# Transposing the probabilities and x by DMA in an attention and feed-forward block, with the products with v between the Q and the K projection

## The reference

```python
x = x + layernorm(attention(layernorm(x), Wq, Wk, Wv, Wo))
x = x + layernorm(ffn(layernorm(x)))
```

## Time and profile before

| | |
|---|---|
| median of 3 runs | 2287.74 us (2286.65 to 2289.22) |
| the profiled execution's own time | 2287.41 us |
| its span, first to last instruction | 2285.6 us |
| TensorE (PE) busy | 2179.5 us, 95% |
| VectorE (DVE) busy | 1384.5 us, 61% |
| ScalarE (ACT) busy | 792.8 us, 35% |
| GpSimd (POOL) busy | 774.8 us, 34% |
| DMA queue of SP, share of 16 engines | 13.7% |

### The profile page before, as it was taken

The page is one execution under the profiler, slowest core; times in us unless marked ns, Lnnn a source line. Parts: engine busy times, 40 slices in busy tenths (PEclk is TensorE's granted clock), DMA queues, the critical chain, the costliest instruction groups (busy, mean ns, idle before and its releaser), DMA issues.

```text
span 2285.6 us, 35735 instructions
## 1 busy us (share of the span) xinstructions
PE 2179.5 (95%) x13184; PEld 1134.0 (50%) x13184; DVE 1384.5 (61%) x3327; ACT 792.8 (35%) x1829; POOL 774.8 (34%) x905
## 2 busy tenths in 40 slices
PE   3989999999999999999999998769999999999997
PEld 2445555555555555555555554434444444444443
DVE  6776676576676676576566575775555455555544
ACT  4544444444444444444444443431111111111111
POOL 0254545545455454554545544610000000000000
PEclk8999999999999999999999999879999999999999
DMA  7000010010010010000010020231121221212111
GB/s 290 2 28 15 19 42 15 20 42 10 26 42 10 24 34 19 25 29 24 16 37 24 10 88 10 85 114 63 49 93 37 93 74 48 82 38 91 38 56 37
DMA packets 31190, 108.73 MB, mean 48 GB/s; under 512 B 4161, under 2 KB 4161, under 8 KB 29986
## 3 DMA queue, kind: packets, MB, share of 16 engines
q1 hardware_dynamic: 31010, 106.34, 13.7%
HBM read 72.77 MB, written 33.55 MB: 47 GB/s over the span
## 4 chain that ended last, share of the span: by engine, by line
PE 91%; DVE 4%; issue 1%; POOL 1%; DMA 1%; ACT 1%; SPq 0%; POOLq 0%; DVEq 0%; ACTq 0%
PE ps L568 29%; PE ps L428 10%; PE ps L429 9%; PE ps L430 9%; PE ps L462 6%; PE ps L453 5%; PE ps L439 5%; PE ps L440 5%; PE ps L441 5%; PE ps L473 5%; PE ps L598 1%; PE ps L558 1%; PE ps L418 1%; POOL arena L1148 1%; DVE arena L719 1%
## 5 line engine op out<-in xcount | busy, mean ns | idle before, releaser
L1148 POOL TENSOR_TENSOR arena<-arena,row_inv 128x512 f32<-128x512 f32 (+3 forms) x512 | 358.3, 737 | 648.7 <-DVE row_inv L730 648.7
L428 PE MATMUL ps<-arena,region 128*128 128x512 f16 x1024 | 389.4, 380 | 0.0
L429 PE MATMUL ps<-arena,region 128*128 128x512 f16 x1024 | 388.5, 379 | 0.0
L430 PE MATMUL ps<-arena,region 128*128 128x512 f16 x1024 | 388.3, 379 | 0.0
L568 PE MATMUL ps<-region 128*128 128x512 f16 x1536 | 341.5, 383 | 8.2 <-ACT arena L1101 4.6
L815 DVE CUSTOM_DVE_ANT_0 arena<-ps,con,pow 128x512 f32<-128x512 f32 (+3 forms) x512 | 246.4, 547 | 161.5 <-PE ps L453 161.5
L568 PE MATMUL ps<-region,arena 128*128 128x512 f16 x1536 | 337.4, 379 | 0.0
L1063 ACT ACTIVATE arena<-arena,neg_max 128x512 f32<-128x512 f32 (+3 forms) x512 | 280.0, 548 | 98.3 <-DVE neg_max L815 98.3
L706 DVE TENSOR_TENSOR rotated<-ps,con 128x512 f32<-128x512 f32 x128 | 88.5, 691 | 267.2 <-PE ps L430 267.2
L568 PEld LDWEIGHTS ps<-region 128*128 128x128 f16 x1536 | 151.3, 99 | 186.5 <-issue 10.1
L568 PEld LDWEIGHTS ps<-region,arena 128*128 128x128 f16 x1536 | 149.1, 98 | 174.2 <-issue 0.8
(11 more groups left out here) (123 smaller groups left out, 2732.8 us busy)
## 6 DMA issues: line engine op xcount, KB each, us to landing
arena<-x SPq DMA_DIRECT2D x32, 512.0 KB, 3.8
attn_scratch<-o_st SPq DMA_DIRECT2D x64, 256.0 KB, 2.2
region<-attn_scratch SPq DMA_DIRECT2D x8, 2048.0 KB, 9.1
v_split<-x SPq DMA_DIRECT2D x32, 512.0 KB, 4.2
out<-v_split SPq DMA_DIRECT2D x32, 512.0 KB, 5.1
arena<-wv SPq DMA_DIRECT2D x4, 1024.0 KB, 13.7
region<-wq SPq DMA_DIRECT2D x4, 1024.0 KB, 18.8
arena<-wk SPq DMA_DIRECT2D x4, 1024.0 KB, 6.6
```

Of the source, the lines that this page charges most:

```text
L428: mm(o, w[:, k, 0, cols], xnt[par][:, k, 0, :], start=(k == 0), stop=False)
L429: mm(o, w[:, k, 0, cols], xnt[par][:, k, 1, :], start=False, stop=False)
L430: last = mm(o, w[:, k, 1, cols], xnt[par][:, k, 0, :], start=False, stop=(k == KT - 1))
L1148: gp.tensor_tensor(unit_sb(j, a), unit_sb(j, a), row_inv[:, n:n + 1].broadcast_to([PART, 128 * (j + 1)]), ALU.mult).then_inc(norm_done, 1)
```

## The change

P and x of the next batch are no longer transposed by TensorE. ACT writes the normalised probabilities' high half (the product with the inverse row sum, which carries the factor 2^14 now), DVE the low half, both as f16 in SBUF; SP then issues one transposing DMA of 128 x 2560 for each half into `pt`. POOL normalises nothing any more. For x, one tile is loaded at a time into `x_tile`, normalised, split, and each half transposed by a DMA. On TensorE the products with v of pair g-1 stand between the Q and the K projection and are cut at the query blocks of the new layout (36 instead of 24 matmuls over the same columns). The order of the query blocks changes. As `x_ring` gives room away, the chunks of W_O and W_F are loaded two at a time, and half of them a second time.

```diff
-Q_ORDER = (3, 2, 0, 1)
+Q_ORDER = (2, 0, 3, 1)
+PV_PIECES = {0: ((0, 2), (2, 2)), 1: ((1, 1), (2, 2)), 2: ((2, 2),), 3: ((3, 1),)}
...
 # SP, slot
+                if not last_b and 1 <= p <= ST:
+                    tok = slice(128 * (p - 1), 128 * p)
+                    for hl, src in enumerate((xn_high_t, xn_low_t[:, :])):
+                        sp.wait_ge(xn_split[hl], n)
+                        if p == 1 and hl == 0 and not first:
+                            sp.wait_ge(qk_done[1], PAIRS * b)
+                        sp.nop(nofuse=True)
+                        sp.dma_start_transpose(xnt[1 - bp][:, :, hl, tok], src).then_inc(xnt_in[hl], 16)
                 if not last_b and p < ST:
-                    sp.wait_ge(xt_done, 8 * b + 2 * p + 2)
-                    sp.dma_start(x_ring[:, p, :], x_v[b + 1, p]).then_inc(x_in[p], 16)
+                    if first and p == 0:
+                        sp.wait_ge(xt_done, 2 * ST)
+                    else:
+                        need(sp, xn_split[1], n)
+                    sp.dma_start(x_tile, x_v[b + 1, p]).then_inc(x_next_in, 16)
+                if not (first and p == 0):
+                    sp.wait_ge(pv_done, g)
+                for hl in range(2):
+                    sp.wait_ge(p_done[hl], 8 * g + 8)
+                    sp.nop(nofuse=True)
+                    sp.dma_start_transpose(pt[:, hl], p_split[:, hl].rearrange("p a n -> p (a n)")).then_inc(
+                        pt_in[hl], 16)
                 if not (first and p == 0):
                     sp.wait_ge(o_low, g)
...
 # TensorE, slot
-                need(pe, pt_low, NG * g)
+                need(pe, masked, 8 * g)
                 need(pe, o_low, g - 1)
                 score_products()
                 qk_product(0, n_pair, n_bp, range(KT), bank)
-                need(pe, masked, 8 * g + 8)
-                if not last_b and 1 <= p <= ST:
-                    need(pe, xn_done, 4 * b + 4 + p)
-                    for hh in range(2):
-                        x_transposes(p - 1, hh, BANK_XT[hh])
+                if not (first and p == 0):
+                    need(pe, masked, 8 * g + 8)
+                    need(pe, v_low, v_before(kind, p, b))
+                    for hl in range(2):
+                        need(pe, pt_in[hl], 16 * g)
+                    pv_products((p - 1) % PAIRS)
                 if has_qk:
                     need(pe, v_low, v_before(kind, p, b))
                     qk_product(1, n_pair, n_bp, range(KT), 1 - bank)
-                if not (first and p == 0):
-                    need(pe, v_low, v_before(kind, p, b))
-                    pv_products((p - 1) % PAIRS)
-                need(pe, norm_done, 8 * g + 8)
-                p_transposes()
...
 # DVE
+            def p_low_part(g, n):
+                j, a = UNITS[n]
+                need(dve, p_done[0], 8 * g + n + 1)
+                v.scalar_tensor_tensor(unit_p(j, a, 1), unit_sb(j, a), row_inv[:, n:n + 1], unit_p(j, a, 0),
+                                       ALU.mult, ALU.subtract).then_inc(p_done[1], 1)
...
                 inverse(g, 0)
+                if not last_b and 1 <= p <= ST:
+                    xn_low_part(4 * b + p - 1)
+                inverse(g, 1)
                 if has_qk:
                     qk_drain(0, g + 1, bank)
-                inverse(g, 1)
+                need(dve, pt_in[1], 16 * g)
+                for n in range(len(UNITS)):
+                    p_low_part(g, n)
                 if not last_b and p < ST:
-                    need(dve, x_in[p], 16 * (b + 2))
-                    ln_stats(p, 4 * b + 4 + p)
+                    need(dve, x_next_in, 16 * (4 * b + p + 1))
+                    ln_stats(p, 4 * b + 4 + p, x_tile)
-                if last_b and p < 2:
+                if last_b and p in (1, 2):
...
                 if has_qk:
                     qk_drain(1, g + 1, 1 - bank)
+                if not last_b and p < ST:
+                    ln_apply(p, 4 * b + 4 + p, x_tile)
+                if has_qk:
                     qk_low_part(0, g + 1)
                 if not (first and p == 0):
                     o_evac(g - 1, (p - 1) % 2)
-                for grp in range(NG):
-                    pt_evac(grp, g)
                 if has_qk:
                     qk_low_part(1, g + 1)
-                if not last_b and p < ST:
-                    ln_apply(p, 4 * b + 4 + p)
...
 # ACT, slot: after the exponentials
-                    for hh in range(2):
-                        xt_evac(p - 1, hh, 1 - bp, 8 * b + 8 + 2 * (p - 1) + hh, BANK_XT[hh])
+                need(act, pt_in[0], 16 * g)
+                for n in range(len(UNITS)):
+                    p_high_part(g, n)
...
-                for grp in range(NG):
-                    pt_evac(grp, g)
+                if not last_b and p < ST:
+                    xn_high_part(4 * b + p)
...
 # POOL, slot
-                for n in range(len(UNITS)):
-                    normalise(g, n)
```

More of the change, by code:

```diff
@@ L307, in unit_sb, with unit_p, raw_of @@
             return scores[:, a, S_OFF[j]:S_OFF[j] + 128 * (j + 1)]
+        def unit_p(j, a, hl):
+            return p_split[:, hl, a, S_OFF[j]:S_OFF[j] + 128 * (j + 1)]
+        def raw_of(w, c, again):
+            if w in w_raw:
+                return w_raw[w][:, KC * c:KC * (c + 1), :]
+            return raw_late[c + 2 if w == W_F and again else c % 2]
         block = ctx.enter_context(nc.Block())
@@ L377, in slot @@
                         store_o(b, p - 1, (p - 1) % 2)
+                if last_b and p == 0:
+                    for c in (0, 1):
+                        load_raw(W_O, c)
+                if last_b and p in (1, 6):
+                    w = {1: W_O, 6: W_F}[p]
+                    for c in (2, 3):
+                        sp.wait_ge(part_max_done, CHUNKS * {W_O: 1, W_F: 2}[w] + c - 1)
+                        load_raw(w, c)
+                if last_b and p == 4:
+                    for n in (0, 1):
+                        sp.wait_ge(w_low_done, CHUNKS * W_O + n + 1)
+                        load_raw(W_O, n, again=True)
+                if last_b and p == 5:
+                    for n in (0, 1):
+                        sp.wait_ge(w_low_done, CHUNKS * W_O + n + 3)
+                        load_raw(W_F, n)
+                if last_b and p == PAIRS - 1:
+                    phase2_loads()
             def batch(b, kind):
@@ L383, in _ @@
             over_batches(sp, batch)
+            for hl in range(2):
+                sp.wait_ge(pt_in[hl], 16 * PAIRS * B)
+            for c in (0, 1):
+                load_raw(W_F, c, again=True)
             sp.wait_ge(o_low, PAIRS * B)
@@ L541, in slot @@
                     if p >= 4:
-                        need(pe, xt_low, 8 * b + 8 + 2 * (p - 4) + 2)
+                        for hl in range(2):
+                            need(pe, xnt_in[hl], 16 * (4 * b + p - 3))
                     v_product(p % 4, 1 if p < 4 else 0, bp if p < 4 else 1 - bp, range(KT), bank)
@@ L549, in _ @@
             over_batches(pe, batch)
-            pe.wait_ge(pt_low, NG * PAIRS * B)
+            for hl in range(2):
+                pe.wait_ge(pt_in[hl], 16 * PAIRS * B)
             pe.wait_ge(o_low, PAIRS * B - 1)
@@ L729, in inverse @@
                 need(dve, exp_done, 8 * g + 4 * part + 4)
-                v.reciprocal(row_inv[:, 4 * part:4 * part + 4], row_sum[:, 4 * part:4 * part + 4]).then_inc(inv_done, 1)
+                four = slice(4 * part, 4 * part + 4)
+                v.reciprocal(row_rec[:, four], row_sum[:, four]).then_inc(recip_done, 1)
+                need(dve, recip_done, 2 * g + part + 1)
+                v.tensor_scalar(row_inv[:, four], row_rec[:, four], P_UP, None, ALU.mult).then_inc(inv_done, 1)
             dve.wait_ge(const_in, 32)
@@ L841, in slot @@
                 if last_b and p in (4, 5):
[L842 to L843 removed]
+                    for n in (0, 1):
+                        split_low(W_O, 2 * (p - 4) + n, LATE_ORDER[2 * (p - 4) + n])
                 if last_b and p >= 6:
@@ L1070, in slot @@
                         act.wait_ge(v_done, 8 * B)
-                    split_high(W_O, 2 * (p - 4))
-                    split_high(W_O, 2 * (p - 4) + 1)
+                    for n in (0, 1):
+                        split_high(W_O, LATE_ORDER[2 * (p - 4) + n], again=p == 5)
                 if has_qk:
@@ L1117, in step @@
                 if kind == 0:
-                    split_high(W_F, 2)
-                    split_high(W_F, 3)
+                    split_high(W_F, LATE_ORDER[2], again=True)
+                    split_high(W_F, LATE_ORDER[3], again=True)
             over_tiles(act, step)
```

153 lines of the change are left out of this document (68 added, 85 removed), and 5 rows, old and new, of the table PT_GROUPS.

## The result

The changed kernel takes 2325.32 us (median of four runs, 2323.25 to 2326.24); the kernel before, run beside it, 2287.19. The ratio is 1.0165, with a 95% interval of 1.0147 to 1.0182: **1.65% slower**, where a gain of 39 us was forecast. The profiled execution took 2325.03 us, its span 2323.2, and the mean granted clock of TensorE is 0.952, where it was 0.979.

A forecast was written before the change was run, and what follows sets the result against it. TensorE's instructions were taken as the bound, with K's tail right behind. Middle slots -53, batch 0 +11 and -6, last batch +4 and +5 sum to -39 us from 2287.41: 2248 us, range 2200 to 2320.

The forecast's parts named there:

- DVE, ACT, POOL: Work moved to these engines: low halves of P some 3.3 us on DVE, beside TensorE, ending at about 12 us.
- The x slots: Slots 0 to 3 of a batch: x work delays K's drain up to 1 us, adding 0.9 us, then 1.3.
- the forecast of the middle slots: Slots 8 to 55: mean slot 20.8 us, a gain of 1.1 us in each of 48, 53 us.
- The term for the clock: Batch 0, slots 0 to 3: after 6 us idle, scores run at the lower clock, 1.74 us more each.
- The tail of K: Drain to rounding and difference after K's product: 6.0 us, covered only by a 5.3 us V product, stalling TensorE 1 us.
- TensorE's own time: TensorE alone per slot: 21.92 less 2.33 and 0.55 for transposes, plus 0.15 for more v instructions, 19.2 us.
- Rival 1: TensorE stays the bound if K's tail is below 5.3 us: slots 19.2 us, about 2170 us; chance 5%.
- Rival 2: Work crowds ahead of K's drain, POOL starting K's rotation 1 us later each slot: about 2295 us; chance 20%.
- Rival 3: Transposing DMAs set the pace through slow small rows, from 8.7 us each: about 3110 or 4850 us; chance 15%.
- packet row: Evidence for slow transposing DMAs: the queue's mean packet of 162 ns, giving an upper bound of 25.8 us per transfer.
- The figure of 5 us: Assumed time of each 640 KB transposing DMA of P, near the plain x load; covered up to 8.7 us.
- The ends: First and last batches: +11 and -6 us in batch 0, +4 and +5 us in the last.

The follow-up runs named there:

- run 5: Changed kernel with v products behind the K projection, POOL's Q rotation after the low halves, x statistics behind K's drain: 2184.80 us, ratio 0.9551.
- run 1: Changed kernel with only the products with v put back behind the K projection: 2320.82 us, ratio 1.0145 to the kernel before.
- run 3: Changed kernel with the x work done in batch 0 alone, leaving out part of the computation: 2237.56 us, ratio 0.9776.
- run 7: Changed kernel with v products behind the K projection and x statistics behind K's drain, POOL still rotating Q beside the low halves: 2227.17 us.
- run 2: Changed kernel with POOL rotating Q only after the low halves of P are done: 2249.50 us, ratio 0.983.
- run 4: Changed kernel with x statistics behind K's drain, the root behind K's rotation, normalisation and high half of x later: 2231.30 us, ratio 0.9753.
- run 6: Changed kernel with Q's rotation after the low halves and x statistics behind K's drain, v products left between Q and K: 2224.46 us.
- run 10: run 5 with the last batch's weight maxima behind K's drain, all-reduce behind K's rotation, next part's clearing ahead of the maxima: 2164.43 us.
- run 8: Changed kernel with the high halves of P transposed twice by DMA, 640 KB more a slot: 2326.77 us, ratio 1.0171.

## Why the prediction was wrong

**The step that failed** is the one headed "DVE, ACT, POOL": the low halves cost "3.06 us, plus three more instructions, some 3.3", and "They lie beside TensorE". They take 5.8 us. They start at 8.4 us of the slot, as the prediction had it (8.5), and end at 14.2, not at 12. So DVE comes to K's drain 13.2 us after its first mask, 14.2 after the scores' start (the first mask follows that by 1.0), just when K's product ends, and whatever else DVE does ahead of the drain delays the tail in full. In x slots the drain was to start up to 1 us late, at 15.1; it starts at 15.8 us in the first x slot of a batch and at 17.4 where the slot begins at the lower clock. Two readings were wrong in the 3.3 us. The 3.06 us came from L719 in the earlier trace rows, which reads one input from PSUM and one from SBUF; L758 reads two from SBUF. Alone it takes 3.77 us (run 5), 0.5 above the estimate. And beside POOL's two rotations, 3.0 us of work there, it takes 5.8 (runs 1, 3, 7). The prediction knew that the two engines hold each other off, from the earlier trace rows, but charged it to POOL alone. The trace of the kernel before had DVE's half too. In the slot of the earlier trace rows the low halves of Q and of K are the same instruction with two SBUF inputs; the first runs beside POOL's rotation of K, the second with POOL idle. The DVE instruction of the earlier trace rows is there again with POOL idle, too:

```profile
612.31 1.13 DVE L713 TENSOR_TENSOR qk_low<-rotated,qk_high 128x512 f16<-128x512 f32 x1 [0.77 <-ACT qk_high L1009]
...
616.95 0.67 DVE L713 TENSOR_TENSOR qk_low<-rotated,qk_high 128x512 f16<-128x512 f32 x1
...
1519.42 4.60 DVE L671 SCALAR_TENSOR_TENSOR region<-arena,pow,region 128x2048 f16<-128x2048 f32 x2
```

That is 1.13 against 0.67 us, and 4.60 us where the earlier trace rows has 5.34 beside the normalisations. The Trainium skill states the rule, in "SBUF — State Buffer" (Who interferes with whom): an exclusive lock on a port pair that DVE and GpSimd share, where the order of issue decides who blocks; a DVE instruction with two SBUF inputs contends with a GpSimd instruction that reads SBUF, and one with at most one SBUF input, outside the 2-port modes, does not. Runs 2 and 7 agree for the two SBUF inputs, 3.77 against 5.80 us; run 5 agrees for the other half, since POOL's pass at 906.18 takes 1.28 us beside L744, which reads PSUM. Who blocks whom no run here separates.

**The x slots**, four of a batch, have a mean of 21.4 us in the forecast and of 23.5 in batches 1 to 6, 51 us in all. Of the 67 us between the forecast of the middle slots and their time this is the largest part; the slot after them (21.2 to 21.9 us, at the lower clock at first) has 8, and two slots at the loop's edge, see the end, most of the rest. The mechanism, statistics ahead of the drain, was in the text at 0.9 and 1.3 us, and measured 2.1 (22.4 against 20.3): 1.6 of it ahead of the drain, 0.5 in a longer tail (7.58 against 7.09 us to the next first mask). The 1.7 us of the statistics were right; that the low halves end without slack made all of them count. The late tail then bared TensorE for 3.0 us and cost it the clock, 1.6 us more in the slot that follows. The term for the clock was there, for four slots of batch 0, and was put at nothing for the x slots of the other batches. Runs 3 and 4 show both, since without the work or with its place changed all of it goes, 88 and 94 us.

**The tail of K**, 6.0 us, and K's end at 14.1 gave 20.2 for a slot without x: 20.3 measured, but by coincidence. DVE's arrival at 14.2 with a tail of 6.1 (7.09 less the 1.0 to the mask) gives 20.3, and so does K's end, which run 6 shows: with the collision gone the slots stay at 20.3. The causes stood one behind the other, two of them within 0.1 us, and each hid what removing the others would give. Hence 4.5 us for the products' place in run 1 and 39.7 in run 6; it takes both to say what a part costs.

**TensorE's own time** came out close. "19.2 us" for TensorE alone stands beside 19.3 us busy in the slot of the kernel after (926.18 to 946.48) and slots of 19.6 in run 5. The 36 products take 1.8 us where 24 took 1.75. The "15,360 columns" given for that are twice the count, 7,680 (1,280 for each of three products and two heads), which changes no term. Rival 1 gave 2170 for a kernel with TensorE as its bound, and runs 5 and 10 took 2185 and 2164; they got there by covering the tail, not by the shorter tail that the rival asked for.

**Rival 2** named what happened, work that crowds ahead of K's drain with the clock lost in x slots, and gave it 20%. Its price, 2295, was 30 us short, because it put the delay at 1 us a slot, at POOL, and left the low halves at their length. It also took the ends at +12 where the forecast's own terms add up to +14.

**Rival 3**, the transfers, fell: run 8. Its packet row was no guide, since 162 ns held for packets of 3.4 KB on the mean, and 256-byte packets cost 24 ns. The figure of 5 us, from the x load, measured 4.9. The Trainium skill's 1309 ns a block ("VectorE: DVE Perf Modes", The three transpose paths) is no pace for a row of blocks: 20 of them land in 4.9 us. Its 1.9 us, estimated in the prediction from "Advanced Engine Details and Errata" (X-Bar Transpose (TRN2)), were meant before the latency, and the runs come out slower: 640 KB hold SP's queue for 3.06 us (median of L383), 214 GB/s, and an estimate from the two sizes, 384 KB more in 1.8 us more (4.9 against 3.1), gives 218 GB/s.

**The ends.** Batch 0 came to +7 where +11 and -6 were forecast. Its bare slots last 22.5 to 24.0 us, forecast 23.1: +13 in these four, and -6 in the other four as forecast. The last batch with the way to the second part came to +19 where +9 was forecast: the low halves at 5.8 us stand ahead of the maxima in four slots and of the splits of W_O in two, and all of these ahead of K's drain. Run 10 removed 20 us there by the order alone, so the order was the cause.

## What to carry to other kernels

When a change moves work to an engine that is not the bound, cost it by a row with the same kinds of operands (which inputs lie in SBUF), and read a collision on both engines. Then write down when each engine arrives at the handover that sets the next step, with the collision in it; arrivals within a few tenths of each other are one bound with several causes, and undoing one of them can show next to nothing (4.5 us in run 1). Work with no hurry, such as the statistics of a tile that only the next batch needs, belongs behind the drain that TensorE waits for.

## What the runs showed of the hardware

- **DVE and POOL slow each other**, and here serialising them is the better order: 3.77 + 2.55 us one after the other in run 5, against 5.8 and 3.0 at once. How the loss is shared differs: here DVE lost 2.0 us and POOL 0.5, in the earlier trace rows POOL lost 4.1 and DVE 0.7.
- **Transposing DMAs with 256-byte rows** moved 640 KB in 4.9 us, at 24 ns a packet on their engine, and cost nothing on the path; with one of them doubled the kernel took 2326.8 instead of 2325.3 us, which is no difference.
- **A wait of 3 us on TensorE** is in most x slots followed by some 3 us at the clock's lower level (granted 0.50 from 880.2 to 883.6), which makes the next slot 1.6 us longer: x slots of 24.0 us, one after the other. Not every such wait does it: in batches 1 and 6 the clock stays up behind the first (3.05 us before 298.35, granted 1.00 up to 306), and the next slot takes 23.0. Behind a wait of 1.0 us the clock stayed up (granted 1.00 from 925.2 to 928.4). The lower clock does not bring the next wait about: it is 3.06 us (831.35) already behind the first x slot of a batch, which had none of it. With few such waits the mean granted clock is 0.974 (run 10), and 0.952 with them.
- **Left open:** the steps into slots 24 and 40 take longer than their neighbours in all versions, 23.5 and 23.8 us from the first mask of slots 23 and 39 against 20.3 in the kernel after, and 21.9 and 22.0 against 21.5 in the kernel before. TensorE and ACT stand idle there without a releaser, 2.4 and 2.7 us in run 4; TensorE at the first scores of slot 24:

```profile
593.93 0.34 PE L493 MATMUL ps<-qk_high 64*128 64x384 f16 x2 [2.40 <-issue]
```

It is where the loop over batches goes back to its start. No run tries the cause; in run 10 these two steps, 24.2 and 24.4 us beside 19.6, still hold some 9 us.
